# A graph network in one kernel: a transformer layer's attention and tail joined to one stage, narrow products moved behind the edge counts, two ramps of the first GAT made ahead, a load cut in pieces

## The reference

```python
def gat_conv(x, src, dst, W, att_src, att_dst, bias, heads, out_ch):
    src, dst = with_loops(src, dst)
    h = (x @ W).reshape(N, heads, out_ch)            # 8 x 128, then 8 x 64
    a_src, a_dst = einsum('nhc,hc->nh', h, att_src), einsum('nhc,hc->nh', h, att_dst)
    e = leaky_relu(a_src[src] + a_dst[dst], 0.2)
    m = segment_max(e, dst)
    ex = exp(e - m[dst])
    alpha = ex / (segment_sum(ex, dst)[dst] + 1e-16)
    return segment_sum(h[src] * alpha[:, :, None], dst).reshape(N, heads * out_ch) + bias
x = layernorm(x + log_softmax(gat_conv(relu(gat_conv(x, ...)), ...)))
for l in range(2):
    q, k, v = ((y @ Wq[l].T + bq[l]) * scaling), y @ Wk[l].T, y @ Wv[l].T
    scores = einsum('ehd,ehd->eh', q[tgt], k[srcidx])
    w = softmax_over_the_edges_of_a_target(scores)
    agg = segment_sum(w[:, :, None] * v[srcidx], tgt)
    y = batchnorm(y + agg @ Wo[l].T + bo[l])
    y = batchnorm(y + relu(y @ W1[l].T + b1[l]) @ W2[l].T + b2[l])
x = layernorm(x + layernorm(y))
```

## Time and profile before

| | us |
|---|---|
| three timed runs | 1684.9, 1680.37, 1683.83 |
| median | 1683.83 |
| the profiled execution | 1682.88 |
| its span | 1681.0 |
| mean granted clock of PE | 0.964 |

### The profile page before, as it was taken

The page is one execution under the profiler, slowest core; times in us unless marked ns, Lnnn a source line. Parts: engine busy times, 40 slices in busy tenths (PEclk is TensorE's granted clock), DMA queues, the critical chain, the costliest instruction groups (busy, mean ns, idle before and its releaser), DMA issues. The chain is left out here.

```text
span 1681.0 us, 35480 instructions
## 1 busy us (share of the span) xinstructions
PE 1538.8 (92%) x14602; PEld 1417.6 (84%) x14602; DVE 1264.6 (75%) x2117; ACT 1160.5 (69%) x2089; POOL 53.9 (3%) x67
## 2 busy tenths in 40 slices
PE   7899799999997788788999999999799999999982
PEld 3788799999985777787988999999799899999982
DVE  5996899989467999996537777776842777777577
ACT  2455688888765899897537888883433788888434
POOL 0000000000000100000000100000300000000030
PEclk9999899999997999999999999999999999999995
DMA  5113222300006221112141211104030021000502
GB/s 184 54 55 105 82 75 72 132 32 2 1 1 164 109 93 63 62 63 76 38 152 56 66 53 32 33 8 137 1 121 1 10 75 32 17 14 2 129 1 61
DMA packets 58515, 103.51 MB, mean 62 GB/s; under 512 B 15569, under 2 KB 33713, under 8 KB 58352
## 3 DMA queue, kind: packets, MB, share of 16 engines
q1 hardware_dynamic: 58352, 101.22, 19.3%
HBM read 75.74 MB, written 19.21 MB: 56 GB/s over the span
## 5 line engine op out<-in xcount | busy, mean ns | idle before, releaser
L2131 DVE CUSTOM_DVE_ANT_0 probs_att<-banks,logs_or_y 125x1250 f32<-125x1250 f32 x160 | 227.3, 1457 | 124.6 <-PE banks L2015 124.1
L1028 PE MATMUL banks<-ident,probs_gat 125*125 125x125 f32 x1600 | 215.8, 285 | 44.1 <-ACT probs_gat L1132 43.4
L1028 PEld LDWEIGHTS banks<-ident,probs_gat 125*125 125x125 f32 x1600 | 196.4, 197 | 54.8 <-ACT probs_gat L1132 54.7
L1132 ACT ACTIVATE probs_gat<-probs_gat,neg_max_gat 125x1250 f32<-125x1250 f32 x160 | 214.7, 1342 | 32.7 <-DVE neg_max_gat L1301 32.3
L1301 DVE CUSTOM_DVE_ANT_0 probs_gat<-probs_gat,log_counts 125x1250 f32<-125x1250 f32 x160 | 236.7, 1480 | 0.1
L2082 ACT COPY probs_t_att<-banks 125x500 f32<-125x500 f32 x400 | 199.4, 597 | 36.3 <-PE banks L2036 36.3
L2074 ACT ACTIVATE probs_att<-probs_att,neg_max_att 125x1250 f32<-125x1250 f32 x160 | 215.7, 1372 | 9.3 <-DVE neg_max_att L2131 9.3
L2036 PE MATMUL banks<-ident,probs_att 125*125 125x125 f32 x1600 | 195.7, 278 | 3.4 <-DVE neg_max_att L2131 3.3
L2036 PEld LDWEIGHTS banks<-ident,probs_att 125*125 125x125 f32 x1600 | 180.7, 188 | 16.9 <-issue 16.4
L2045 PE MATMUL banks<-probs_t_att,v_rows 125*64 125x125 f32 x3200 | 189.0, 272 | 1.8 <-ACT probs_t_att L2082 1.8
L1039 PE MATMUL banks<-h,probs_t_gat 125*125 125x128 f32 x1600 | 188.0, 273 | 0.0
(11 more groups left out here) (258 smaller groups left out, 2868.1 us busy)
## 6 DMA issues: line engine op xcount, KB each, us to landing
a_pair<-a_src_rows SPq DMA_DIRECT2D x46, 625.0 KB, 4.8
logs_or_y<-log_rows SPq DMA_DIRECT2D x20, 546.9 KB
w_rows<-in_L_gnn_W_dram SPq DMA_DIRECT2D x12, 512.0 KB, 6.7
log_counts<-counts_fr SPq DMA_DIRECT2D x50, 122.1 KB
x_cols<-feature_cols SPq DMA_DIRECT2D x2, 2500.0 KB
logs_or_y<-x_cols SPq DMA_DIRECT2D x10, 500.0 KB, 5.2
x_rows_sb<-in_x_dram SPq DMA_DIRECT2D x1, 2240.0 KB
x_rows<-x_rows_sb SPq DMA_DIRECT2D x10, 224.0 KB
```

The source lines that it names most:

```text
L1028: block_t = pe.transpose(turned(u)[:, i // 2, (i % 2) * P:(i % 2 + 1) * P], probs[:, u % PROBS, i * P:(i + 1) * P], k.ident[0:P, 0:P])
L1132: act.activation(probs[:, u % PROBS], probs[:, u % PROBS], ACT.Exp, scale=-1.0, bias=neg_max[:, column(u)], accum_out=sums[:, column(u)]). ...
L2131: dve.tensor_tensor_reduce(probs[:, u % SLOTS], scores(u % 2), logs[:, t % KEPT], -1.0, -FLOOR, ALU.add, ALU.min, neg_max[:, column(u)]).t ...
```

## The change

It has seven parts.

1. In stage_front each head of weigh_atts follows a count of its own, in steps 1 to 8. Its save by ACT, the turn, the logits and the cuts of w move behind (WEIGH, LOGITS, CUT, LOWER). START stays. wa_turned gets a buffer of its own. On DVE, place_atts goes behind the one-hots of step 0.
2. At the end of stage_front DVE makes the ramps of units 0 and 1 into a buffer of their own (early_probs).
3. In the second GAT, units 0 and 1 get 1000 of 1250 columns of their ramp and mask ahead of weigh_atts(9) (first_parts). The other 250 follow at their old place, and a minimum joins the two parts' results.
4. The x rows are loaded in five pieces of two tiles, behind the pair loads of parts 3 to 7, and wk behind that of part 8.
5. lower_next goes from Pool to DVE, to the end of the stage. The casts (cut_next) move from the first part of layer 2 to units 120, 124, 128 and 132.
6. safe and invert work on four units in place of two.
7. Attention and tail become one stage per layer, stage_layer. The tail's x_cols are loaded once all of the 80 masks are done, the next weights once the heads are weighed, and ACT makes the first cut of the tail, cut_tail(0), between two of the last saves of the attention.

The diff, cut to its core:

```diff
@@ stage_front
-    CUT = 2
-    LOWER = 3
-    LOGITS = 1
+    WEIGH = 1
+    CUT = 9
+    LOWER = 10
+    LOGITS = WEIGH + H + 1
     START = 15
...
-        wa_turned = counts[0:DST + H, 1].rearrange("p g w -> p (g w)")[:, 0:K * 128]
+        wa_turned = sb("wa_turned", [DST + H, K * 128])
...
+            dve.wait_ge(dst_saved, 1)
+            dve.wait_ge(gat.spread[0], 32)
+            for u in range(gat.EARLY_RAMPS):
+                dve.scalar_tensor_tensor(gat.early_probs[:, u], gat.pair[0:P, 0, 0], gat.gap1[:, u, 0:1], gat.pair[0:P, 0, 1],
+                                         ALU.add, ALU.max)
...
-            save_wa_rows()
             for s in range(STEPS):
                 if s < G:
                     save_group(s)
-                if s == 0:
+                if s == WEIGH + H - 1:
+                    save_wa_rows()
+                if s == WEIGH + H:
                     save_wa()
...
-            def weigh_atts():
+            def weigh_att(head):
+                if head == 0:
                     pe.wait_ge(w_turned_loaded, 16)
                     pe.wait_ge(att_placed, 1)
-                for head in range(H):
@@ stage_gat
             load_pair(1, 1)
-            for a, b in row_parts(P):
-                sp.dma_start(gat.y[a:b], x.rearrange("(t p) d -> p t d", p=P)[a:b]).then_inc(rows_loaded, 16)
-            sp.dma_start(next_w[0][:], next_source).then_inc(next_loaded, 16)
             for part in range(2, 2 * H):
-                sp.wait_ge(ramp_done, first_unit(part - 1))
+                sp.wait_ge(ramp_done, first_unit(part - 1) - OWN)
                 load_pair(1, part % H)
-            sp.wait_ge(rows_loaded, 32)
+                i = part - ROWS_FROM
+                if 0 <= i < T // 2:
+                    tiles = slice(2 * i, 2 * i + 2)
+                    for a, b in row_parts(P):
+                        sp.dma_start(gat.y[a:b, tiles], x.rearrange("(t p) d -> p t d", p=P)[a:b, tiles]).then_inc(rows_loaded, 16)
+                if part == NEXT_FROM:
+                    sp.dma_start(next_w[0][:], next_source).then_inc(next_loaded, 16)
...
-        @block.gpsimd
-        def _(pool):
-            for c in range(NEXT):
-                pool.wait_ge(next_high_done, c + 1)
-                pool.tensor_tensor(next_w[2][:, c], next_w[0][:, c], next_w[1][:, c].bitcast(F32), ALU.subtract).then_inc(next_low_done, 1)
...
+            def first_parts():
+                dve.wait_ge(dst_done, OWN)
+                dve.tensor_scalar(gap2[:, 0:OWN], a_all[:, 0:OWN, 1], 1.0 - NEG_SLOPE, None, ALU.mult).then_inc(gap_done, 1)
+                dve.wait_ge(spread_saved, len(spans) - 1)
+                dve.wait_ge(gap_done, 1)
+                dve.wait_ge(probs_turned, PER - PROBS + OWN)
+                for u in range(PER, PER + OWN):
+                    make_ramp(u, 0, spans[-1][0]).then_inc(part_ramped, 1)
+                for i, u in enumerate(range(PER, PER + OWN)):
+                    dve.wait_ge(part_ramped, i + 1)
+                    make_mask(u, 0, spans[-1][0], part_max[:, i:i + 1]).then_inc(part_masked, 1)
...
-                    if live(1, n - 1) and n % 2 == 0:
-                        safe_pair(n - 2)
+                    if live(1, n - 1) and n % 4 == 0:
+                        safe_four(n - 4)
...
+            def lower_next(c):
+                dve.wait_ge(next_high_done, c + 1)
+                dve.tensor_tensor(next_w[2][:, c], next_w[0][:, c], next_w[1][:, c].bitcast(F32), ALU.subtract).then_inc(next_low_done, 1)
...
             attend(1)
+            for c in range(NEXT):
+                lower_next(c)
@@ attention and tail
             if p == PAIRS + 1:
                 save_turned(p - 2)
+                cut_tail(0)
             if p >= 3:
                 save_att(p - 3)
...
+    def tail_sync(sp):
         sp.dma_start(bias_o[:], bo.rearrange("(c p) -> p c", p=128), allow_slow_non_contiguous=True).then_inc(bias_loaded, 16)
+        sp.wait_ge(k.cols_stored, 16)
+        sp.wait_ge(k.masked, T * k.H)
         for i in range(CHUNKS):
             sp.dma_start(y[:, :, nodes(i)], x_cols.rearrange("(c p) n -> p c n", p=128)[:, :, nodes(i)]).then_inc(x_loaded[i], 16)
...
+        sp.wait_ge(k.heads_weighed, T * k.H // 2)
         for j, ((rows, _, _), source) in enumerate(zip(next_weights, next_sources)):
...
+            if s == 0:
+                act.wait_ge(k.scored, T * k.H // 2)
+            if s < CHUNKS:
+                act.wait_ge(k.att_saved, (s + 1) * k.H)
...
+def stage_layer(k, places, projected, attended, closed):
+
+    with k.stage(f"stage_layer{k.layer}") as ctx:
+        project_sync, project_tensor, project_scalar, project_vector = project_parts(k, ctx, places, *projected)
+        attend_sync, attend_tensor, attend_scalar, attend_vector, attend_gpsimd = attend_parts(k, ctx, places, *attended)
+        tail_sync, tail_tensor, tail_scalar, tail_vector, tail_gpsimd = tail_parts(k, ctx, places, *closed)
+        block = ctx.enter_context(k.nc.Block(f"layer{k.layer}"))
...
```

734 lines of the change are left out of this document (382 added, 352 removed).

## The result

The changed kernel takes 1654.14 us (median of 4 runs, 1653.34 to 1655.18), the kernel before 1684.23 in the same comparison (4 runs, 1680.37 to 1684.9). The ratio is 0.9826, with a 95% interval of 0.9809 to 0.9843: 30 us faster. The forecast was 1650 in a range of 1642 to 1662. The profiled execution took 1655.18 us with a span of 1653.2, 27.8 less than the 1681.0 of before.

A forecast was written before the change was run, and what follows sets the result against it. PE, busy 1538.8 of 1681.0 us, was the bound, with DVE and ACT setting the second GAT's pace. Terms 8.5 + 2.9 + 3.4 + 5.0 + 4.3 + 2.2 + 8.0 = 34.3 gave 1650 us, range 1642 to 1662.

The forecast's parts named there:

- Front: Front: counts start at about 11.4 with one head behind each of steps 1 to 8; count(15) at 56.2, gain 8.5 us.
- Rival A: Front: low clock or ACT's long queue replaces the old wait, so 8.5 becomes about 1; 1657 us, chance 0.20.
- Ramps ahead: First GAT's start: two ramps leave the chain and go into DVE's idle time, gain 2.9 us.
- First parts: Second GAT's start: early ramps and masks fill DVE's 4.84 us wait; third mask ends at about 527.5, gain 3.4 us.
- Loads: Second GAT: with the next pair issued first, DVE's 4.98 us wait goes and none follows, gain 5.0 us.
- Rival C: Second GAT loads: first pair still waits or pieces delay later pairs; gain 0 to 1, 1654 us, chance 0.05.
- Pool to DVE: Second GAT: four masks each lose 1.08 us of lengthening; DVE's subtractions fall in idle time, gain 4.3 us.
- Fours: Second GAT: safe and invert by fours takes DVE from 2.88 to 2.84 per unit, gain 2.2 us.
- Joins: Attention to tail, two places: PE's wait and the following slow products go, 4.0 us each, gain 8.0 us.
- Rival B: Second GAT: ACT becomes the bound, so the 4.3 and the 2.2 go; 1656 us, chance 0.14.
- Rival D: Second GAT: PE at its low clock costs 2.0 us per unit; 25 units give about 1698 us, chance 0.03.
- The forecast's own sign: Whole kernel: the prediction is wrong if any PE stretch that was at 1.00 falls under 0.9.

The follow-up runs named there:

- cuts_early: Changed kernel with wk loaded behind the pair of part 2 and its casts on ACT at units 92 to 104: 1652.07 us.
- two_early: Changed kernel with two heads behind each of counts 1 to 4, and cuts, subtractions, logits and projection start four steps earlier: 1652.25 us.
- whole_rows: Changed kernel with the x rows loaded in one piece behind the pair of part 2: 1654.15 us.
- front_alone: Kernel before with only the front's new order, without early ramps: 1676.98 us against 1685.49.
- joins_alone: Kernel before with part 7 alone, attention and tail in one stage per layer: 1677.76 us against 1685.49.
- no_first: Changed kernel without the first parts of units 80 and 81, both made whole at their old place: 1655.8 us.
- pool_early: As cuts_early, but with the four subtractions on Pool right behind the casts: 1656.74 us.
- pairs: Changed kernel with safe and invert for two units at once in place of four: 1655.68 us.
- after_again: Changed kernel profiled once more with no edit: 1654.16 us, span 1651.1.

## Why the prediction was right, and where its terms were off

The forecast of 34.3 us stands against 30.1 by the medians and 27.8 in the profiled execution, inside the range, and the mechanisms were in the main those that were named. By stage the 27.8 are 6.5 for 8.5 in the front, 4.1 for 2.9 in the first GAT, 10.0 for 14.9 in the second, 7.9 for 8.0 at the joins, and 0.7 lost behind them. Term by term:

- *Front, 8.5; measured 6.5* (projection at 59.54, not 57.5). The chain over ACT did set it, as forecast, but it began later. Its rows in the changed kernel:

```profile
34.86 0.58 ACT L478 COPY wa_turned_fr<-banks 40x512 f32<-40x512 f32 x1 [0.51 <-PE banks L562]
...
50.39 1.03 ACT L519 CAST w_high<-w_rows 128x1024 fp32r<-128x1024 f32 x1
...
51.46 1.22 DVE L402 TENSOR_TENSOR w_low<-w_rows,w_high 128x1024 fp32r<-128x1024 f32 x1 [0.49 <-ACT w_high L519]
...
55.94 1.00 DVE L370 TENSOR_TENSOR key_hot_fr<-node_row,group_keys 125x1638 bf16<-125x1638 f16 x1
```

  The forecast let ACT's queue start at 32.0, behind count(7) and eight heads. The last head stands behind count(8), and a count with a head has a pitch of 2.53 (1.55 and 0.98), not 2.19, so the queue starts at 34.86. From there to the end of the fourth cast it takes 16.6, not 18.5, and DVE behind it 5.5, not 5.4. So the keys of count(15) are there at 56.94, 0.7 later than the 56.2. The other 1.3 are Rival A in a small form: PE was at the low clock in these two counts, so count(15) started only at 57.46 and lasted 2.08, not 1.34. In other executions the same time goes at the start: the last two counts took 4.39 us in the changed kernel and 3.26 in cuts_early, the first two 4.35 and 5.57. The floor of PE was too low as well, by 2.7 us over the eight steps and 0.8 over the four behind them, but with them it is 55.6 and still not the last to come.
- *Ramps ahead, 2.9; measured 4.1.* The two ramps are as forecast: the exponential of unit 1 gains 3.0 over the start of the stage. What was missing is PE's clock. Before, PE works at half of its clock up to 186, as the windows of the kernel before show:

```profile
182.00:186.00 4.00, 2.89 (x12) 2.61 (x13) 4.00 (x8) 3.65 (x6) 0.00 (x0) 0.50 0.00 0
186.00:190.00 4.00, 4.00 (x31) 4.00 (x31) 4.00 (x9) 3.12 (x4) 0.00 (x0) 0.78 0.00 0
```

After, PE is up from 175 on, 8 us into the stage and not 12 to 14. The windows of the changed kernel:

```profile
171.00:175.00 4.00, 4.00 (x19) 3.87 (x20) 4.00 (x8) 3.10 (x4) 0.00 (x0) 0.50 0.22 77
175.00:179.00 4.00, 3.40 (x30) 3.21 (x30) 4.00 (x8) 3.58 (x6) 0.00 (x0) 0.99 0.00 0
```

  The extra gain, 1.0 between units 2 and 6, is not secure: nine of the eleven traces with early ramps have it, but in two_early and whole_rows PE comes up 3 to 4 us later and they lose 0.5 and 0.4 there. The traces with the old start of the stage differ too: front_alone and joins_alone lose 0.6 and 1.0 against the kernel before. That the early work brings the clock up sooner is likely, but not shown apart from such chance.

- *First parts, 3.4; measured 3.4 to 3.8* with the clock up (no_first), and 2.05 in the profiled execution, where PE's low clock delayed tile 9 and with it DVE. The changed kernel then gave back 0.9 at unit 83 to a wait for the pair, which the prediction had not priced: what comes earlier asks for its data earlier.
- *Loads, 5.0; measured 5.0* (units 83 to 87, in all traces 4.8 to 5.2). Rival C is false. Right size, but for the order alone.
- *Pool to DVE, 4.3; measured 4.3* in the trace and 4.7 by medians (pool_early). DVE's subtractions at the end take 2.47 us of an idle time that is still 7.71 behind them. The casts on ACT, which the prediction moved for free, cost 0.6 at their new place and some 0.4 net.
- *Fours, 2.2; measured 1.2 to 1.3* (pairs).
- *The end of the second GAT, where the forecast had no loss.* From unit 131 to 159 the lead falls by 1.4 (2.1 in after_again). ACT's roots stand there, between two table loads of 1.28 us each (at 694.29 and 695.81); PE waits for the exponentials behind them, the clock is 0.83 over 700 to 710, and DVE waits for PE's turned probabilities for 2.25 us in three rows, against one of 1.11 in the kernel before. The longest of each, in the changed kernel and before:

```profile
707.54 1.52 DVE L1303 SCALAR_TENSOR_TENSOR probs_gat<-a_pair,a_dst_gap_gat 125x1250 f32<-125x1250 f32 x1 [1.14 <-PE banks L1054]
```

```profile
722.30 1.52 DVE L1295 SCALAR_TENSOR_TENSOR probs_gat<-a_pair,a_dst_gap_gat 125x1250 f32<-125x1250 f32 x1 [1.11 <-PE banks L1028]
```

- *Joins, 8.0; measured 7.9*, of which about 0.5 is lost again at the end of each tail (joins_alone). But the low clock behind a join, 1.6 of each 4.0, is not sure to come: front_alone had one join without it. So part of the 7.9 rests on how the execution of the kernel before fell out.
- *Rival B* is false where it was placed: ACT is busy for 82.45 of 85 us at 535 to 620 while DVE has all 85.00, so DVE keeps the pace with 3% to spare on ACT. In a small form it is true later, at the casts and the roots.
- *Rival D* is false: in 620 to 752 the clock is 0.96. But the condition was read rightly; the dips of some us are its small form. The forecast's own sign, no stretch of PE falling from 1.00 to under 0.9, did show at 499 to 503 (0.57; the same work in the kernel before, at 509 to 513, has 1.00), and in after_again it didn't. Its other sign, that the second GAT shrinks by 10 or more, was met with nothing to spare (10.0).

So the sum was 4 us too high against the medians. Its largest error is the second GAT's 4.9: 1.4 at the first parts by the low clock, a pair asked for sooner (0.9), fours (0.9), late casts (0.4 to 0.6) and the loss at its end (1.4) had no price or too high a one. In after_again, with the clock up at tile 9, it is 2.9. The front's error is 2.0, the start of ACT's queue and the low clock, and the ramps err by 1.2 the other way. That the total came out near the forecast is thus in part luck: the clock's gain at the ramps, which was not foreseen, stands against its losses elsewhere. Two slips of arithmetic change nothing: the terms of ACT's queue give 50.35, not 50.5, and the joins' bound of 9 lies 1.0 above 8.0, not 1.3.
